# Score units inside the projections, four output chunks inside the score stream: one attention and feed-forward layer on one core

## The chip, the cores and the metric

The kernel runs on one core of a Trainium2 chip. The metric is the device time of one execution in microseconds (us): the median of three runs. Everything below that is not a median comes from one further execution, which the hardware profiler recorded.

## The reference

The input x has 2 sequences of 2048 rows and 256 channels; there are 16 heads of 16 channels. Cut to what matters:

```
q_in = x Wq' + b;  Q = [q_in, conv3(q_in)] proj_q' + b        # k likewise, V = x Wv' + b
tau, delta = sigmoid(conv1(gelu(depthwise_conv3(x))))         # one value per head and row
scores = (Q K' / 4) * tau + delta                             # 2 x 16 x 2048 x 2048
out    = softmax(scores) V;  x1 = layernorm(x + out Wo' + bo)
xq     = mxfp4_round(x1);    y  = layernorm(x1 + xq mxfp4_round(W)' + bf)
```

The rounding divides each block of 32 channels by a power of two taken from the block's largest value, clips to 6, rounds to a 4-bit float and multiplies back. It works on rows of x1, so a row needs all 16 heads first.

## The kernel before, in words

Rows are cut into 8 chunks of 512 (`NCHUNK`), chunks 0 to 3 of sequence 0 and 4 to 7 of sequence 1. Heads go in 8 groups of four (`NG`); an iteration is one group and one chunk of query rows, 32 iterations (`NIT`), those of sequence 1 from 16 on. Chunk n of the output is complete when its four groups are: chunk 3 with iteration 15, chunks 4, 5, 6 and 7 with iterations 28, 29, 30 and 31.

**The first block: projections** (`n` from 0 to 7). Convolution and projections are folded into one set of weights. For each chunk TensorE makes k in two halves, v in two, q in two (`project`, L608, 18 matmuls a half; `values`, L619), and the `pointwise` matmuls of tau and delta (L628) for the chunk after. VectorE adds the outer taps of the depthwise convolution (`tap`, L440), 16 instructions a chunk, between ScalarE's middle tap (L382) and gelu (L388). An fp32 operand is kept as a high part and a low part (`high`, `low`; L83 and L87): ScalarE writes the high parts of x, q and delta, VectorE the low ones (`split_low`, `q_lows` and one for delta). SyncE stores k, q and delta to DRAM and loads the first head group back.

**The score stream.** Softmax needs each row's maximum before its exponentials. So every score is made twice: once as a *unit*, a pair of matmuls into two PSUM banks (`s_unit`, L208) that VectorE reduces to maxima (`max_unit`, L218), and once transposed (`st`, L833) for ScalarE's exponential (L989) and the product with v (`pv_half`, L846). An iteration has 32 units. The list `items` holds all units in order, and after the third unit of each iteration one item `rows`, which turns the maxima of the iteration before (L820, L1024), for SyncE to store into `q_set` (`rows_store`, L797). Items use two pairs of banks in turn, so that item s waits on TensorE for the reduction of item s-2 (`s_free`). GpSimd splits the maxima (`split_max`).

Of `items`, `PRE_STEP` puts 28 into the projections of chunks 4 to 7; TensorE runs the next 17 at the start of the second block, each with six matmuls whose result nobody reads (L914), and only then the first `st`. From there, `due` items are spread over the 32 half-steps of an iteration, 33 in each of iterations 0 to 29 and 22 in the first 24 half-steps of iteration 30. I call a half-step a *slot*: one `pv_half`, one pair of `st`, and its item or items.

**Last iteration and tail.** From the third-last k tile of iteration 30 on, TensorE makes the output rows of chunks 0 to 3 (`project`, 16 *blocks* of 128 rows, L866 to L869). VectorE takes their layernorm statistics (`moments`, L1059, L1063), ScalarE a square root (L948), VectorE normalises (L1107) and rounds (`scales`, `steps`, `rounds`, L1080 to L1097). After the last `pv_half`, for n = 0 to 7: TensorE transposes the rounded chunk n (L884), projects chunk n+4, and multiplies with the feed-forward weights (`linear`, L904); ScalarE evacuates (`turn`, L971) and normalises twice (`norm`, L958). SyncE loads each chunk (`chunk_load`, L713 to L722: its rows of x, the attention of four groups, the reciprocals of the softmax sums) once the one two before has been used, and GpSimd multiplies the attention by the reciprocals (`normalise`, L1179). Every engine and every DMA queue takes its instructions in the order in which the code issues them.

```
for s in range(PRE, lead_in):
    s_item(s)
    for m in range(WARM):
        ...
issued = lead_in
for i in range(NIT):
    due = min(PER, len(items) - issued)
```

## Time and profile before

| | us |
|---|---|
| median of three runs | 1694.66 (1692.73 to 1697.91) |
| profiled execution, its own time | 1700.33 |
| its span, first to last instruction | 1698.5 |
| TensorE matmul busy | 1642.5 (97%) |
| VectorE busy | 1538.2 (91%) |
| ScalarE busy | 1322.7 (78%) |
| GpSimd busy | 74.6 (4%) |

How to read it: the profiled execution took 1.8 us outside its span, and is 5.7 us above the median. Shares of busy time are averages over stages with different limits. Times in rows are counted from the first instruction. The program has one core, and its mean granted TensorE clock is 0.981 of full speed.

### The profile page before, as it was taken

Reading aid. Unit: us, or ns where it says so; the run is one execution under the profiler, and the core shown is the slowest. Engines: PE = TensorE matmul, PEld = TensorE weight load, DVE = VectorE, ACT = ScalarE, POOL = GpSimd, SP = SyncE. Lnnn points to the kernel's source line nnn. Section 1 sums busy time; section 2 is a strip of 40 time slices with the busy share of each in tenths; the row PEclk is TensorE's granted clock in tenths of the full one; section 3 lists DMA queues with packets and bytes.
Section 4 is the critical chain, followed back from the end, with each engine's and each line's share of the span. In section 5 each row is a group of like instructions: output and inputs, shape, how many; then the busy total and the mean of one; then the engine's idle time right before and its main releaser. Section 6 shows DMA issues by size and latency. Waiting matters only on the chain.

```text
span 1698.5 us, 33654 instructions
## 1 busy us (share of the span) xinstructions
PE 1642.5 (97%) x13972; PEld 745.1 (44%) x13978; DVE 1538.2 (91%) x1638; ACT 1322.7 (78%) x2389; POOL 74.6 (4%) x133
## 2 busy tenths in 40 slices
PE   8999989999999999999999999999999999998977
PEld 7677754333333333333333333333333333334466
DVE  5588977999999999999999999999999999985797
ACT  3688723888888888888888888888888888885534
POOL 3000003000000000000000000000000000001110
PEclk9899997999999999999999999999999999999998
DMA  3376436000600060006002400322050000002232
GB/s 111 91 191 171 123 91 95 9 8 8 76 16 8 8 84 8 8 9 83 8 14 30 66 8 8 51 44 61 29 71 21 8 8 8 8 8 86 82 101 75
DMA packets 46961, 84.73 MB, mean 50 GB/s; under 512 B 9116, under 2 KB 21020, under 8 KB 44092
## 3 DMA queue, kind: packets, MB, share of 16 engines
q1 hardware_dynamic: 44952, 82.49, 22.6%
q8 instruction: 110, 1.80, 0.5%
q14 instruction: 43, 0.35, 0.1%
q10 hardware_dynamic: 1856, 0.09, 0.1%
HBM read 51.36 MB, written 30.67 MB: 48 GB/s over the span
## 4 chain that ended last, share of the span: by engine, by line
PE 62%; DVE 21%; ACT 1%; issue 1%; ACTq 0%; POOL 0%; DVEq 0%
PE ps L846 26%; PE ps L833 20%; DVE mx L218 17%; PE ps L208 11%; PE ps L869 1%; PE ps L914 1%; PE ps L867 1%; PE ps L820 0%; DVE stats L1059 0%; DVE work L1094 0%; DVE work L1093 0%; ACT e L989 0%; DVE work L1085 0%; DVE small L1080 0%; DVE scr L1089 0%
## 5 line engine op out<-in xcount | busy, mean ns | idle before, releaser
L218 DVE TENSOR_REDUCE mx<-ps 128x2 f32<-128x1024 f32 x1024 | 1230.4, 1223 | 60.6 <-PE ps L208 51.2
L989 ACT ACTIVATE e<-ps 128x512 f32<-128x512 f32 x2048 | 1110.3, 596 | 210.5 <-PE ps L833 170.4
L846 PE MATMUL ps<-e,v_grp 128*32 128x256 f32 x8192 | 657.7, 393 | 0.2 <-issue 0.2
L833 PE MATMUL ps<-q,k 52*128 52x512 f32 x2048 | 525.3, 499 | 4.0 <-ACT e L989 4.0
L208 PE MATMUL ps<-k,q 50*128 50x512 f32 x2048 | 420.8, 404 | 11.1 <-DVE mx L218 6.5
L833 PEld LDWEIGHTS ps<-q,k 52*128 52x128 f32 x2048 | 199.4, 184 | 430.8 <-ACT e L989 400.0
L846 PEld LDWEIGHTS ps<-e,v_grp 128*32 128x32 f32 x8192 | 162.1, 108 | 359.2 <-issue 202.4
L208 PEld LDWEIGHTS ps<-k,q 50*128 50x128 f32 x2048 | 198.9, 188 | 39.7 <-DVE mx L218 31.0
L608 PE MATMUL ps<-x_p,m_p 128*128 128x512 f32 x576 | 143.1, 405 | 0.0
L608 PEld LDWEIGHTS ps<-x_p,m_p 128*128 128x128 f32 x576 | 109.1, 193 | 31.0 <-issue 6.5
L440 DVE SCALAR_TENSOR_TENSOR hid<-x_c,dw_w,hid 128x512 f32<-128x512 f32 x128 | 88.5, 746 | 13.2 <-ACT hid L382 13.2
L388 ACT ACTIVATE hid<-hid 128x512 f32<-128x512 f32 x64 | 40.5, 633 | 41.4 <-DVE hid L440 40.0
L83 POOL CAST nm_pad<-nm 128x16 fp32r<-128x16 f32 x32 | 6.7, 209 | 923.1 <-DVE nm L1035 923.1
L382 ACT ACTIVATE hid<-x_c,dw_b,dw_w 128x512 f32<-128x512 f32 x64 | 46.6, 804 | 0.2
L1059 DVE BATCH_NORM_STATS2 stats<-ps 128x6 f32<-128x256 f32 x64 | 23.5, 419 | 21.9 <-PE ps L869 17.6
L869 PE MATMUL ps<-wo_t,v_all 128*128 128x256 f32 x128 | 36.7, 414 | 0.0
L628 PE MATMUL ps<-hid,pw_w 128*16 128x512 f32 x128 | 31.2, 594 | 0.2 <-ACT hid L388 0.2
L431 ACT ACTIVATE q_sp<-qx 128x512 fp32r<-128x512 f32 x16 | 10.1, 631 | 26.3 <-DVE qx L468 26.1
L619 PE MATMUL ps<-wv_p,x_p 128*128 128x256 f32 x192 | 27.1, 292 | 2.0 <-DVE v_all L458 2.0
L869 PEld LDWEIGHTS ps<-wo_t,v_all 128*128 128x128 f32 x128 | 26.8, 209 | 4.4
L958 ACT ACTIVATE o_sb<-ps,shift,rstd 128x256 f32<-128x256 f32 x32 | 15.5, 563 | 16.6 <-DVE shift L1071 16.6
L619 PEld LDWEIGHTS ps<-wv_p,x_p 128*128 128x128 f32 x192 | 25.7, 197 | 4.4 <-DVE v_all L458 2.1
(127 smaller groups left out, 621.8 us busy)
## 6 DMA issues: line engine op xcount, KB each, us to landing
k<-k_parts SPq DMA_DIRECT2D x42, 256.0 KB
q<-q_parts SPq DMA_DIRECT2D x42, 256.0 KB
k_parts<-k_sp SPq DMA_DIRECT2D x16, 512.0 KB, 5.1
q_parts<-q_sp SPq DMA_DIRECT2D x16, 512.0 KB, 4.6
att<-ev SPq DMA_DIRECT2D x32, 256.0 KB
x_c<-in_x_t SPq DMA_DIRECT2D x8, 514.0 KB, 6.4
tau_r<-tau_rows SPq DMA_DIRECT2D x16, 256.0 KB
x_in<-in_x SPq DMA_DIRECT2D x8, 512.0 KB, 3.7
```

Source lines behind the costliest of these rows:

```text
L208: last = nc.tensor.matmul(ps[:, s_bank(s) + half, :], q_set[r, g % 2, jh, lo + qt * P:lo + (qt + 1) * P], k_set[r, g % 2, jh, kc * CH:(kc ...
L218: nc.vector.tensor_reduce(mx[:, j % 2, :, jh, qt, kc], ps[:, b0:b0 + 2, :], AX.X, ALU.max).then_inc(s_free, 1)
L382: nc.scalar.activation(hid[:, k, c, r], x_c[:, n % 2, c, 1:1 + CH], ACT.Identity, bias=dw_b[:, k, c, r:r + 1], scale=dw_w[:, k, c, r, 1:2] ...
L388: nc.scalar.activation(hid[:, k, c, r], hid[:, k, c, r], ACT.Gelu).then_inc(gelu_done, 1)
L440: nc.vector.scalar_tensor_tensor(y_, x_c[:, n % 2, c, which:which + CH], dw_w[:, k, c, r, which:which + 1], y_, ALU.mult, ALU.add).then_in ...
L608: last = nc.tensor.matmul(ps[:, o, :], m_p[:, kw, side, c, tap, P * o:P * (o + 1)], x_p[:, n % 2, kx_, c, tap:tap + CH], start=(m == 0), s ...
L619: last = nc.tensor.matmul(ps[:, V_BANK, D * a:D * (a + 1)], x_p[:, n % 2, kx_, c, lo:lo + P], wv_p[:, kw, c, :], start=(m == 0), stop=(m = ...
L628: last = nc.tensor.matmul(ps[32 * k:32 * k + H, TD_BANK, :], pw_w[:, k, 2 * c + r, :], hid[:, k, c, r, :], start=(j < 2), stop=(j >= 6))
L833: nc.tensor.matmul(ps[:, st_bank(n), :], k_set[r, g % 2, jh, kt * P:(kt + 1) * P], q_set[r, g % 2, jh, lo:lo + CH], start=True, stop=True) ...
L846: last = nc.tensor.matmul(ps[32 * h:32 * (h + 1), 0, PVW * part:PVW * (part + 1)], v_grp[:, kt, h, :], e[:, x % E_BUFS, h * CH + PVW * par ...
L869: last = nc.tensor.matmul(dst, a_t[p][:, c, P * a:P * (a + 1)], wo_t[:, c, :], start=False, stop=(c == CT - 1))
L989: nc.scalar.activation(e[:, x % E_BUFS, h * CH:(h + 1) * CH], ps[:, st_bank(n), :], ACT.Exp).then_inc(e_ready, 1)
```

## The change

It does five things.

1. The units of iteration 0 are taken in another order (all of the first 512 keys, then the next 512, `place_of`), beginning in chunk 2; each group of 512 keys waits for its own loads. `PRE_STEP` now puts 42 items into the projections: 5 in chunk 2, 6 in each of chunks 3 to 6, and 13 in chunk 7, where they also stand between the matmuls of a half. The turn of iteration 0's maxima is among them. The separate lead-in of 17 items and its unread matmuls are gone: 14 go to the projections and 3 into iteration 0.
2. The low parts of x, q and delta are made by GpSimd.
3. The 16 blocks of chunks 0 to 3 become items: four in each of iterations 28 to 31 of the list, which the stream reaches in iterations 26 to 30. VectorE copies each from PSUM to `y_of`, and takes the statistics from there after the last item. Chunks 4 and 5 are projected in the last iteration in eight steps; chunks 6 and 7 after `linear(0)` and `linear(2)`.
4. ScalarE takes the square roots of chunks 0 to 3 together before the last iteration's first exponential, and a fourth set of softmax sums (`Z_SETS`) lets chunks 4 and 5 be loaded during iteration 31. Twenty unread matmuls stand at the end of iteration 30.
5. In chunk 0 the first values are evacuated after VectorE's other work, and the second ones have a bank of their own. SyncE waits for the stores of the first block in the second.

```diff
+        O_AT = {(28 + n, 8 * a + 5): ("o", n, a) for n in range(4) for a in range(TT)}
...
+        def place_of(j, u):
+            if j == 0:
+                return u % (HH * TT) // HH, u % HH, u // (HH * TT)
+            return u // (HH * NQ), u // NQ % HH, u % NQ
...
-        V_BANK, TD_BANK = 2, 3
+        v_bank = lambda n, v: 5 if (n, v) == (0, 1) else 2
...
-        PRE_STEP = {4: (0, 0, 0, 0, 0, 0, 2), 5: (0, 0, 1, 1, 1, 1, 1), 6: (0, 0, 1, 1, 1, 1, 1), 7: (2, 2, 2, 2, 2, 2, 4)}
+        PRE_STEP = {2: ONE_EACH(6, 9, 10, 13, 14)} | {n: ONE_EACH(5, 6, 9, 10, 13, 14) for n in range(3, 7)} | {7: [1] * 13 + [0, 0]}
...
+                for n in range(NCHUNK):
+                    if n + 1 < NCHUNK:
+                        split_low(n + 1)
+                    if n == NCHUNK - 1:
+                        split_max(pool, 0)
+                        pool.wait_ge(nm_ready, 1)
+                    pool.wait_ge(d_high, n + 1)
+                    low(nc.gpsimd, d_sp[32:32 + H, 1], td[32:32 + H], d_sp[32:32 + H, 0]).then_inc(d_split, 1)
...
+                    for o in range(CT):
+                        pool.wait_ge(q_high, CT * n + o + 1)
+                        low(nc.gpsimd, q_sp[:, o, 1], qx[:, o], q_sp[:, o, 0]).then_inc(q_split, 1)
...
-            PROJECT_AT = [LAST - 3, LAST - 3, LAST - 2, LAST - 2] + [LAST - 1 + m for m in range(3 * TT)]
-            ROOT_AT = {LAST + 1: 0, LAST + 5: 1, LAST + 10: 2}
+            PROJECT_AT = {x0 + a: (n, a) for n, x0 in ((4, LAST + 5), (5, LAST + 10)) for a in range(TT)}
+            ROOT_AT = {LAST - 1: range(EARLY)}
+            WARM_AT = (LAST - 2, LAST - 1)
...
+                            block_of(ps[:, s_bank(s), 0:D], n % 2, a).then_inc(s_full, 1)
...
+                        if s == len(items) - 1:
+                            pe.wait_ge(s_free, s - 1)
+                            unread(s_bank(s), 4)
...
-                    for s in range(PRE, lead_in):
-                        s_item(s)
-                        for m in range(WARM):
-                            for half in range(2):
-                                r = rows_of(half, K_S)
-                                nc.tensor.matmul(ps[:, st_bank(half), :], q_set[r, 0, 0, 0:P], k_set[r, 0, 0, 0:CH], start=True, stop=True)
...
-                        due = min(PER, len(items) - issued)
-                        slots = SLOTS if due == PER else SLOTS * 3 // 4
+                        goal = items.index((i + 2, LEAD)) if i + 2 < NIT else len(items) - 1
+                        due = goal - issued
+                        slots = SLOTS * 3 // 4 if i == NIT - 2 else SLOTS
...
                     for n in range(NCHUNK):
                         transposed(n)
-                        if n + EARLY < NCHUNK:
-                            for a in range(TT):
-                                project(n + EARLY, a)
                         linear(n)
+                        if n in (0, 2):
+                            for a in range(TT):
+                                project(6 + n // 2, a)
...
+                                nc.vector.tensor_copy(y_of[n][:, a], ps[:, s_bank(s), 0:D]).then_inc(s_free, 1)
...
+                        if i == NIT - 1:
+                            z_store(sp, 1)
+                            next_load(4)
+                            next_load(5)
                         if i > 0:
                             att_store(i - 1)
...
                     sp.wait_ge(att_stored, 32 * (NIT - 1))
-                    z_load(sp, 1)
-                    next_load(2)
-                    next_load(3)
-                    z_store(sp, 1)
-                    next_load(4)
-                    next_load(5)
+                    z_load(sp, 2)
+                    z_store(sp, 2)
                     att_store(NIT - 1)
                     next_load(6)
```

What this does to the order of instructions is shown at three places. The first is TensorE in the projections of chunk 3: the rows from one `pointwise` (16x512) to the next, before and with the change. `k,q` rows are score units.

```order
L628 MATMUL ps<-hid,pw_w 16x512 x8
L608 MATMUL ps<-x_p,m_p 128x512 x36
L619 MATMUL ps<-wv_p,x_p 128x256 x12
L608 MATMUL ps<-x_p,m_p 128x512 x18
L619 MATMUL ps<-wv_p,x_p 128x256 x12
L608 MATMUL ps<-x_p,m_p 128x512 x18
```

```order
L705 MATMUL ps<-hid,pw_w 16x512 x8
L225 MATMUL ps<-k,q 128x512 x2
L682 MATMUL ps<-x_p,m_p 128x512 x36
L225 MATMUL ps<-k,q 128x512 x2
L696 MATMUL ps<-wv_p,x_p 128x256 x12
L225 MATMUL ps<-k,q 128x512 x2
L682 MATMUL ps<-x_p,m_p 128x512 x18
L225 MATMUL ps<-k,q 128x512 x2
L696 MATMUL ps<-wv_p,x_p 128x256 x12
L225 MATMUL ps<-k,q 128x512 x2
L682 MATMUL ps<-x_p,m_p 128x512 x18
L225 MATMUL ps<-k,q 128x512 x2
```

A unit now follows each stage of the chunk; the work itself stands where it stood. The second place is VectorE in the same stage, from one group of four taps on its second half to q (`hid` are taps, `mx` reductions of units, L87 low parts): before in chunk 5, then with the change.

```order
L87 TENSOR_TENSOR x_p<-x_c,x_p 128x1028
L440 SCALAR_TENSOR_TENSOR hid<-x_c,dw_w,hid 128x512 x4
L218 TENSOR_REDUCE mx<-ps 128x2
L458 TENSOR_TENSOR v_all<-ps,bv_bc 128x32x16
L218 TENSOR_REDUCE mx<-ps 128x2
L440 SCALAR_TENSOR_TENSOR hid<-x_c,dw_w,hid 128x512 x4
L87 TENSOR_TENSOR d_sp<-td,d_sp 16x512
L468 SCALAR_TENSOR_TENSOR qx<-ps,side_bias,tau_r 128x512
L218 TENSOR_REDUCE mx<-ps 128x2
L468 SCALAR_TENSOR_TENSOR qx<-ps,side_bias,tau_r 128x512
L87 TENSOR_TENSOR q_sp<-qx,q_sp 128x512 x2
L218 TENSOR_REDUCE mx<-ps 128x2
```

```order
L523 SCALAR_TENSOR_TENSOR hid<-x_c,dw_w,hid 128x512 x4
L235 TENSOR_REDUCE mx<-ps 128x2
L537 TENSOR_TENSOR v_all<-ps,bv_bc 128x32x16
L235 TENSOR_REDUCE mx<-ps 128x2
L523 SCALAR_TENSOR_TENSOR hid<-x_c,dw_w,hid 128x512 x4
L547 SCALAR_TENSOR_TENSOR qx<-ps,side_bias,tau_r 128x512
L235 TENSOR_REDUCE mx<-ps 128x2
L547 SCALAR_TENSOR_TENSOR qx<-ps,side_bias,tau_r 128x512
L235 TENSOR_REDUCE mx<-ps 128x2
```

The four low parts have left VectorE; GpSimd has them in the order x (of the next chunk), delta, q, q. The third place is SyncE's queue around the end of iteration 31, with what each row waits for, with the change.

```order
L1313 DMA att<-ev 128x512 [waits att_evac]
L1315 DMA z_rows<-ev 4x512
L790 DMA x_in<-in_x 128x4x256 [waits o_full]
L795 DMA v_all<-att 64x1x512 x4
L799 DMA v_all<-rz_rows 128x1x512 [waits z_stored2]
L799 DMA v_all<-rz_rows 128x1x512
L775 DMA z<-z_rows 128x64 [waits att_stored]
```

The load of chunk 6 (L790 to L799) stands behind the store of iteration 31's result (L1313), as it did before; the loads of chunks 4 and 5 now stand well ahead of both. And at the same point TensorE's rows from the last matmuls of `linear(0)` (L988) on, with the change:

```order
L988 MATMUL ps<-fw_p,xq_t 128x256 [waits t_evac]
L988 MATMUL ps<-fw_p,xq_t 128x256 x7
L866 MATMUL ps<-bias,ones 128x256 [waits y_ready,a_norm,x_in_loaded0]
L867 MATMUL ps<-x_in,ident_f 128x256
L869 MATMUL ps<-wo_t,v_all 128x256 x2
```

The first block of chunk 6 (L866 to L869; three more follow) stands right behind `linear(0)`, ahead of the transposition of chunk 1, and waits for its own load (`a_norm`).

## Rows read from the trace of the kernel before

**Rows 1.** By stage: length, busy PE, PEld, DVE, ACT, POOL; clock, DMA share, GB/s
```profile
74.50:247.70 173.20, 171.80 (x816) 122.87 (x816) 143.58 (x201) 121.71 (x171) 0.00 (x0) 1.00 0.54 145
256.20:275.90 19.70, 19.49 (x133) 13.74 (x135) 17.59 (x18) 1.28 (x1) 14.34 (x25) 0.89 0.45 82
275.90:1529.00 1253.10, 1247.67 (x11855) 466.14 (x11853) 1200.53 (x1060) 1083.74 (x2006) 25.96 (x91) 0.99 0.18 28
1529.00:1604.50 75.50, 68.40 (x504) 34.33 (x496) 48.46 (x88) 47.33 (x83) 11.70 (x5) 0.98 0.27 87
1604.50:1698.50 94.00, 68.01 (x382) 57.84 (x384) 77.52 (x187) 35.07 (x79) 7.11 (x3) 0.87 0.25 85
```

**Rows 2.** Timeline around chunk 0: start, length, engine, line [idle before, releaser]
```profile
58.94 0.69 DVE L458 TENSOR_TENSOR v_all<-ps,bv_bc 128x512 f32<-128x512 f32 x1 [12.51 <-POOL v_all L352]
59.69 2.93 PE L619 MATMUL ps<-wv_p,x_p 128*128 128x256 f32 x12 [1.97 <-DVE v_all L458]
...
74.51 8.66 PE L608 MATMUL ps<-x_p,m_p 128*128 128x512 f32 x36
```

**Rows 3.** TensorE's timeline: starts of chunks 2, 3, 5 and 6
```profile
97.89 8.65 PE L608 MATMUL ps<-x_p,m_p 128*128 128x512 f32 x36
121.23 8.67 PE L608 MATMUL ps<-x_p,m_p 128*128 128x512 f32 x36
...
168.63 8.68 PE L608 MATMUL ps<-x_p,m_p 128*128 128x512 f32 x36
...
194.78 8.65 PE L608 MATMUL ps<-x_p,m_p 128*128 128x512 f32 x36
```

**Rows 4.** VectorE's groups: count, busy us and mean ns
```profile
L440 DVE SCALAR_TENSOR_TENSOR hid<-x_c,dw_w,hid 128x512 f32<-128x512 f32 x128 | 88.5, 746 | 13.2 <-ACT hid L382 13.2
...
L87 DVE TENSOR_TENSOR x_p<-x_c,x_p 128x1028 fp32r<-128x1028 f32 x8 | 9.8, 1225 | 1.2 <-ACT x_p L376 1.2
```

**Rows 5.** GpSimd and VectorE at the same time, timeline
```profile
1570.38 2.36 POOL L1179 TENSOR_TENSOR v_all<-v_all 128x1024 f32<-128x1024 f32 x1 [6.64 <-DMA v_all<-rz_rows]
1570.81 3.01 DVE L1085 TENSOR_TENSOR work<-y,small 128x1024 f32<-128x1024 f32 x1
```

**Rows 6.** TensorE in the stream: starts of a single slot, a double one and the next
```profile
1251.63 0.64 PE L846 MATMUL ps<-e,v_grp 128*32 128x256 f32 x8
...
1252.87 0.64 PE L846 MATMUL ps<-e,v_grp 128*32 128x256 f32 x8
...
1254.69 0.64 PE L846 MATMUL ps<-e,v_grp 128*32 128x256 f32 x8
```

**Rows 7.** TensorE: first and second block of chunk 0 (first matmul of each)
```profile
1533.15 0.28 PE L866 MATMUL ps<-bias,ones 128*128 128x256 bf16 x1
...
1534.57 0.27 PE L866 MATMUL ps<-bias,ones 128*128 128x256 bf16 x1
```

**Rows 8.** TensorE in iteration 31: two slots of a k tile without block, next tile
```profile
1597.95 0.64 PE L846 MATMUL ps<-e,v_grp 128*32 128x256 f32 x8
...
1598.95 0.64 PE L846 MATMUL ps<-e,v_grp 128*32 128x256 f32 x8
...
1600.18 0.64 PE L846 MATMUL ps<-e,v_grp 128*32 128x256 f32 x8
```

**Rows 9.** ScalarE's timeline: the first of two table loads around a root
```profile
1544.96 1.28 ACT L948 ACT_TABLE_LOAD   x1
```

**Rows 10.** The last chunk's load: SyncE's first DMA, GpSimd, TensorE's first block
```profile
1633.69 0.43 SPq L713 DMA_DIRECT2D x_in<-in_x  x1
...
1646.22 2.35 POOL L1179 TENSOR_TENSOR v_all<-v_all 128x1024 f32<-128x1024 f32 x1 [16.53 <-DMA v_all<-rz_rows]
...
1639.39 0.36 PE L866 MATMUL ps<-bias,ones 128*128 128x256 bf16 x1 [4.71 <-ACT y L958]
...
1646.91 1.03 PE L898 MATMUL ps<-v_all,ident_f 128*128 128x256 f32 x4
```

**Rows 11.** Busy time in the stretch at half clock after the first exponentials
```profile
281.00:294.00 13.00, 13.00 (x76) 4.24 (x79) 7.39 (x7) 6.67 (x13) 0.00 (x0) 0.50 1.03 122
```

More of the change, by code:

```diff
@@ L633, in pre_scores @@
                     for s in pre_at.get((n, place), ()):
-                        s_unit(pe, s)
+                        if items[s][1] == "rows":
+                            rows_turn(pe, s)
+                        else:
+                            s_unit(pe, s)
                 beta(1, 0)
@@ L802, in _, with block_of, loaded, unread @@
                 def _(pe):
+                    def block_of(dst, p, a):
+                        nc.tensor.matmul(dst, ones3[:], bias3[:, 0, 0, :], start=True, stop=False)
+                        nc.tensor.matmul(dst, ident_f[:], x_in[:, p, a, :], start=False, stop=False)
+                        for c in range(CT):
+                            last = nc.tensor.matmul(dst, a_t[p][:, c, P * a:P * (a + 1)], wo_t[:, c, :], start=False, stop=(c == CT - 1))
+                        return last
+                    def loaded(n):
+                        pe.wait_ge(x_in_loaded[n % 2], 16 * (n // 2 + 1))
+                        pe.wait_ge(a_norm, n + 1)
+                    def unread(bank, pairs):
+                        for m in range(pairs):
+                            for half in range(2):
+                                r = rows_of(half, K_S)
+                                nc.tensor.matmul(ps[:, bank + half, :], q_set[r, (NG - 1) % 2, 0, 0:P], k_set[r, (NG - 1) % 2, 0, 0:CH], start=True, stop=True)
                     def s_item(s):
                         j, u = items[s]
+                        if isinstance(u, tuple):
+                            n, a = u[1:]
+                            pe.wait_ge(s_free, s - 1)
+                            if a == 0:
+                                loaded(n)
+                            if (n, a) == (0, 0):
+                                pe.wait_ge(bias_ready, 1)
+                            block_of(ps[:, s_bank(s), 0:D], n % 2, a).then_inc(s_full, 1)
+                            return
                         if u == "ft":
@@ L931, in _ @@
                                     issued += 1
[L932 to L935 removed]
+                                if i == NIT - 2 and 2 * k + jh == slots:
+                                    s_item(len(items) - 1)
+                            if x in PROJECT_AT:
+                                project(*PROJECT_AT[x])
+                            if x in WARM_AT:
+                                pe.wait_ge(s_free, len(items))
+                                unread(4, 3)
                     for n in range(NCHUNK):
                         transposed(n)
[L939 removed]
+                        linear(n)
+                        if n in (0, 2):
                             for a in range(TT):
[L941 to L942 removed]
+                                project(6 + n // 2, a)
                 @block.scalar
@@ L1138, in _ @@
+                    for n in range(6, NCHUNK):
+                        moments(1, n)
                         scale_shift(1, n)
@@ L1195, in _ @@
                                 refill(g + 1, c)
-                    for n in range(NCHUNK):
+                    for n in range(EARLY, NCHUNK):
                         normalise(n)
```

407 lines of the change are left out of this document (232 added, 175 removed).

## The prediction, made before the changed kernel was run

> **What bounds the kernel now.** I read the stages first, in the answer that sums each engine's work by stretch [rows 1]. In the projections (74.5 to 247.7) TensorE is busy 171.8 of 173.2 us and VectorE 143.6: TensorE sets the pace. Then comes the lead-in, 19.7 us before the first exponential. In the stream VectorE has 1200.5 of 1253.1 us and TensorE 1247.7, so both are full. From 1529.0, the copy of the last maxima, to the last product with v at 1604.5, VectorE works 48.5 of 75.5 us. In the tail of 94.0 us it works 77.5, the most of any engine. Next I took the starts of TensorE's pieces from the timeline, since a start to start distance holds the waits. A slot with one item takes 1.24 us, one with two 1.83 [rows 6], of which I put 0.15 down to a wait for VectorE, whose two reductions fall into one slot there (my choice; no row splits it). 31 x 1.24 + 1.83 = 40.3 is one iteration. VectorE has 33 items of 1.22 there, some 40.0 in all. What is added to TensorE in the stream therefore shows in full, and what is taken from VectorE does not.
>
> **Chunk 0.** VectorE stands 12.5 us before the first values, and TensorE 2.0 behind it [rows 2]. Both waits go. TensorE gains at least the 2.0. VectorE's taps for chunk 1 come some 6 us sooner, so the last tau and delta matmuls stop waiting for gelu. I take chunk 1 to start at 70.8 instead of 74.5. Ends: 72.5 and 69.5.
>
> **Units in the projections.** A chunk without units takes 121.2 - 97.9 = 23.3 us, one with five 194.8 - 168.6 = 26.15 [rows 3], so a unit costs 0.57. Chunk 7 ran with 14 units from 220.9 (one chunk after 194.8) to 247.7, 26.8 us; with 13 some 26.3. Chunk 1 then ends at 94.1, chunk 2 at 120.2, chunks 3 to 6 take 4 x 26.7 and end at 227.0, chunk 7 at 253.3. One q evacuation, one high and one low part, and the change of block follow, 3.4 us. The first `st` comes at 256.7 instead of 275.9: **-19.2**. Three items move to iteration 0, each between 0.6 (TensorE, 1.83 - 1.24) and 1.22 (VectorE); I take 1.0, as VectorE is nearer to its limit there: **+3.0**.
>
> The units are hidden from VectorE only if it keeps up. A chunk costs it some 19.3 us without units, 16 x 0.746 of it taps. The low parts go: x 1.23 [rows 4], and by their columns 0.7 each for delta and both q, 3.3 together. Six reductions of 1.17 to 1.22 come: 23.2 of 26.7. GpSimd gets them in return. Its two-input instruction over 1024 columns takes 2.36 us [rows 5], so a chunk gives it about 2.4 + 3 x 1.3 = 6.3. When it ran at 1570.4, VectorE's instruction with two SBUF inputs took 3.01 us instead of 1.2 and ended 1.1 after GpSimd's [rows 5]: it had stood still. VectorE's 16 taps have two SBUF inputs too. By the order of the streams x's low part falls on reductions and evacuations, delta's on the second taps, q's on reductions. I take 2 us a chunk as lost, which the 3.5 of slack hold. The Trainium skill, SBUF — State Buffer, section Who interferes with whom, says it as a rule: a VectorE instruction with two SBUF inputs and a GpSimd one that reads SBUF exclude each other for their whole length, a reduction never. By that rule, with all overlaps at their worst, this change would lose time; the trace agrees with the exclusion.
>
> **Blocks in the stream.** A block is 1534.57 - 1533.15 = 1.42 us of TensorE [rows 7], and VectorE's copy of 256 columns some 0.4. 16 x 1.42 = 22.7. The items push others together: 37 items in 32 slots make five double slots instead of one, four times the difference between 1.68 and 1.24 less what four slots without unit save (1.00 instead of 1.24, [rows 8]), about 0.8 an iteration; together 2.8 over the iterations 26 to 30: **+25.5**. Low end 22.7. High end: after a block VectorE has at most one item waiting, and stands up to 2.1 us until the next unit; at 16 x 2.1 it is 34. Five more unread pairs and one slot before the last turn of maxima, of which TensorE waited 1.2 for GpSimd anyway: **+1.8**. The last copy of maxima then ends 11.1 us later than now, at 1540.1.
>
> **From there to the last product.** Now it is 75.5 us. With the change ScalarE takes four roots before iteration 31's exponentials. VectorE needs 1.0 for the reciprocals and four times 1.8 for statistics, so the last root comes at 8.4 and, after a table load of 1.28 [rows 9], the first exponential at 9.7 after the copy. TensorE stops at 5.3, when the three banks of `st` are full, and goes on at 10.3. The end of iteration 30 with its unread matmuls, partly at half clock after the stop, reaches 16.7. Iteration 31 has 14 k tiles of 2.23 [rows 8], two of 1.05 and eight blocks of 1.5: 45.5. Sum 62.2: **-13.3**. VectorE has rounded chunks 0 to 3 by 64.9; it waits some 7 us in it for chunks 4 and 5.
>
> **The tail.** VectorE starts one chunk ahead of where it is now, but new waits eat this. The load of chunk 6 is issued after iteration 31's result is stored, 1.8 us after the last product. From a load's first DMA to GpSimd's product are 12.5 us, that takes 2.35, four blocks after an idle time 7.5 [rows 10], transposition and `linear(1)` 4.5. So the statistics of chunk 1 are due 28.6 us into the tail, where VectorE arrives at 20: what is late next is that load. Chunk 7's blocks stand behind the normalised chunk 6 and ahead of `linear(3)`: another 5. With two waits of 2 us for `norm`, the chunks 4 to 7 need 17 + 21 + 22 + 17 = 77 us from 2.7 on, and the last feed-forward chain 13.4: 93.1 instead of 94.0, **-0.9**.
>
> Sum: -19.2 + 3.0 + 25.5 + 1.8 - 13.3 - 0.9 = -3.1. I round to **-4**, because in chunk 0 the clock may return sooner when TensorE is not idle. The profiled execution would go from 1700.3 to about 1696 (span 1694.5); it stood 5.7 above the median, so the median is 1694.7 - 4 = **1690.5**. A measurement of this kernel can tell 0.3%, 5.1 us, from no change, so this is just inside.
>
> **Rivals.**
> - *The tail has no new waits* (chance 0.20). If the load lands sooner, or VectorE arrives later, the idle 8.6 and 5 go: -4 - 14 = -18, 1677. For it: VectorE does work 77.5 of 94 us now. Against it: the measured 12.5 us of the load.
> - *VectorE and GpSimd exclude each other in the projections* (0.12), slower. If all 6.3 us of GpSimd stop taps, VectorE's chain of taps, gelu, tau and delta, middle taps (some 25 us) becomes 31.5 instead of the 26.7 of TensorE: 4.8 in each of five chunks, +24, net +20, 1711 to 1715. It decides from 4 us a chunk on. For it: 3.01 instead of 1.2. Against it: most of GpSimd's work falls on reductions.
> - *Blocks cost VectorE's time as well* (0.10): the high end of 34, net +4.5, 1699.
> - *The clock* (0.08). For 13 us after the first exponentials it is granted at 0.50, the lower of its two levels, 1.2 GHz [rows 11], and the tail's mean is 0.87 [rows 1]. TensorE stops for 3.4 us at 253 and 5 at 1545. If it stays at 1.2 GHz longer than now, 5 to 12 us are lost: 1695 to 1703. It could also be shorter by 5.
> - *The change does not do what it says*: if units in the projections waited for VectorE instead of filling in, the lead-in would only have moved. That is the second rival in another form, and has its price.
>
> **How the numbers follow.** The sum's case has 0.50, from -10 to +2 by the ends of chunk 0, the units and the blocks: 0.21 of it faster by over 0.3%, 0.27 within, 0.02 slower. The others add 0.20, 0 and 0; 0, 0 and 0.12; 0, 0.06 and 0.04; 0.03, 0.01 and 0.04. Together faster 0.44, same 0.34, slower 0.22. The range 1672 to 1706 takes in the first rival with the better ends of the sum, the third and the clock, and leaves out most of the second. The sum's own range is 1684 to 1697.
>
> **What would show it.** First `st` near 257, TensorE gapless in chunks 1 to 7 and 26.7 a chunk; iterations 27 to 29 of 47 us instead of 40.3; the last copy of maxima near 1540; last product 62 after it; then VectorE idle for 8 us before the statistics of chunk 1. A chunk of 28 or more, with TensorE waiting for gelu or a reduction, would prove the exclusion. Wrong would be a tail under 85 us, or blocks that cost 1.0 or 2.0 each.

## The result: 1% slower, and the profile after

| | before | changed |
|---|---|---|
| median of nine runs, us | 1695.94 (1692.73 to 1705.17) | 1715.56 (1708.43 to 1723.67) |
| ratio | 1 | 1.0098, 95% interval 1.0069 to 1.0127 |
| the same, timed again with the experiments | 1 | 1.0071, 1.0045 to 1.0097 |
| span of the profiled execution | 1698.5 | 1713.8 |

By the two ratios the kernel became slower by 12 to 17 us, where 4 us were forecast as a gain; its median of 1715.56 us lies above the end of the range that I gave, 1706. Busy time by stage of the changed kernel, cut at the places that answer to those of before [rows 1]; the columns are the same, and the gap between the two blocks has a line of its own. The stages are: the start of chunk 1 to the last projection; the gap; the first score to the last copy of maxima; from there to the last product with v; and the tail:

```profile
71.76:255.90 184.14, 184.12 (x852) 125.56 (x851) 154.30 (x191) 120.69 (x170) 45.10 (x30) 1.00 0.50 137
255.90:259.70 3.80, 0.00 (x0) 0.03 (x1) 0.88 (x2) 2.12 (x3) 1.30 (x2) 0.94 0.34 92
259.70:1548.07 1288.37, 1282.06 (x11987) 487.45 (x11987) 1204.80 (x1078) 1084.55 (x2008) 48.64 (x117) 0.99 0.18 32
1548.07:1618.13 70.06, 65.11 (x451) 27.70 (x444) 56.06 (x120) 41.17 (x77) 5.21 (x2) 0.78 0.17 52
1618.13:1713.80 95.67, 55.23 (x329) 46.13 (x328) 62.69 (x156) 35.63 (x78) 4.71 (x2) 0.84 0.24 81
```

Read it against the forecast. TensorE is without a gap in the projections (184.12 of 184.14), as forecast. The stream takes 1288.4 instead of 1253.1: 35.3 more, where 30.3 were forecast. The stage behind it has a mean clock of 0.78 where it had 0.98 before, and takes 70.1 us instead of the forecast 62.2. VectorE has 15 us less work in the tail than before, and the tail is still 1.7 us longer.

The starts of chunks 3, 4 and 5 in TensorE's timeline [rows 3 for before]:

```profile
148.10 8.66 PE L682 MATMUL ps<-x_p,m_p 128*128 128x512 f32 x36
174.85 8.70 PE L682 MATMUL ps<-x_p,m_p 128*128 128x512 f32 x36
201.69 8.66 PE L682 MATMUL ps<-x_p,m_p 128*128 128x512 f32 x36
```

26.8 us for a chunk with six units, forecast 26.7. VectorE's taps in the group of that line [rows 4 for before]:

```profile
L523 DVE SCALAR_TENSOR_TENSOR hid<-x_c,dw_w,hid 128x512 f32<-128x512 f32 x128 | 103.8, 862 | 21.2 <-ACT hid L464 21.2
```

They take 0.862 instead of 0.746 us each, 15.3 us in all or 1.9 a chunk. In one chunk, VectorE's timeline shows it in a single place:

```profile
213.22 1.22 DVE L235 TENSOR_REDUCE mx<-ps 128x2 f32<-128x1024 f32 x1
214.35 4.59 DVE L523 SCALAR_TENSOR_TENSOR hid<-x_c,dw_w,hid 128x512 f32<-128x512 f32 x4
```

GpSimd's timeline at the same time:

```profile
212.96 2.41 POOL L87 TENSOR_TENSOR x_p<-x_c,x_p 128x1028 fp32r<-128x1028 f32 x1 [10.36 <-ACT x_p L458]
215.45 1.62 POOL L87 TENSOR_TENSOR d_sp<-td,d_sp 16x512 fp32r<-16x512 f32 x1
```

Four taps take 4.59 us where four others of the chunk take 2.87, and until 217.07 GpSimd writes the low parts of x and of delta beside them. The exclusion is there, at the 2 us a chunk that I had put down, and it is hidden.

A block in the stream, in TensorE's timeline and then in VectorE's (the last block of chunk 0, [rows 7] for a block before):

```profile
1443.17 0.28 PE L866 MATMUL ps<-bias,ones 128*128 128x256 bf16 x1
1443.29 0.60 PE L867 MATMUL ps<-x_in,ident_f 128*128 128x256 f32 x2
1443.73 1.03 PE L869 MATMUL ps<-wo_t,v_all 128*128 128x256 f32 x4
1444.68 0.64 PE L936 MATMUL ps<-e,v_grp 128*32 128x256 f32 x8
...
1444.79 0.42 DVE L1114 COPY y<-ps 128x256 f32<-128x256 f32 x1 [1.27 <-PE ps L869]
1446.03 2.36 DVE L235 TENSOR_REDUCE mx<-ps 128x2 f32<-128x1024 f32 x2 [0.82 <-PE ps L225]
```

The block takes TensorE 1.5 us (1443.17 to 1444.68), and VectorE stands 1.27 before its copy and 0.82 behind it. In the whole iteration (1415.24 to 1462.93) VectorE works 39.6 of 47.7 us and TensorE 47.3, so TensorE sets the pace. By ScalarE's copies of a finished iteration (1367.56, 1415.24, 1462.93, 1510.66), iterations 27 to 29 take 47.7 us each, against 40.3 without blocks.

The worst place is the end of the stream. ScalarE's timeline, and TensorE's at the same time:

```profile
1548.79 3.27 ACT L1070 ACTIVATE e<-ps 128x512 f32<-128x512 f32 x6 [1.39 <-PE ps L923]
1552.08 1.28 ACT L1030 ACT_TABLE_LOAD   x1
1553.37 0.48 ACT L1030 ACTIVATE std<-mv,eps_col 128x4 f32<-128x4 f32 x2
1554.04 0.30 ACT L1030 ACTIVATE std<-mv,eps_col 128x4 f32<-128x4 f32 x1 [0.18 <-DVE mv L1165]
1555.74 0.30 ACT L1030 ACTIVATE std<-mv,eps_col 128x4 f32<-128x4 f32 x1 [1.40 <-DVE mv L1165]
1556.06 1.28 ACT L1070 ACT_TABLE_LOAD   x1
```

```profile
1552.87 0.50 PE L923 MATMUL ps<-q,k 52*128 52x512 f32 x1
1558.00 0.79 PE L923 MATMUL ps<-q,k 52*128 52x512 f32 x1 [4.62 <-ACT e L1070]
1558.00 2.07 PE L882 MATMUL ps<-k,q 50*128 50x512 f32 x6
```

ScalarE loads a table, takes four roots (the last waits for VectorE's statistics) and loads the table back: 5.3 us. TensorE stops for 4.62 us at the score matmul that needs a free bank. Of the twenty unread matmuls, twelve stand behind that score matmul in the program and come after the stop (the first six at 1558.00). Two stretches in which TensorE runs at the lower clock (same columns as the stages):

```profile
260.00:278.00 18.00, 17.74 (x90) 6.17 (x90) 7.22 (x6) 10.56 (x20) 10.85 (x19) 0.50 0.86 165
1558.00:1585.60 27.60, 27.60 (x154) 8.87 (x155) 26.56 (x38) 16.03 (x30) 5.21 (x2) 0.50 0.31 94
```

In the second, 27.6 us long, the granted clock is 0.50, the lower level of 1.2 GHz, while TensorE is busy without a gap. It stays there until 1587.0, which is 29.0 us after the stop. The first stretch, behind the first score, lasts from 259.3 to 279.8. Neither was in my sum at this length. What the lower level costs is seen in the starts of two k tiles of iteration 31: 3.47 us apart at 0.50 (1566.48 and 1569.95). At 1.00 it was 2.23 before [rows 8], and 2.24 in e2 below (1558.85 and 1561.09).

In the tail, TensorE's two long waits, SyncE's two entries about the load of chunk 6, and GpSimd's product of chunk 6 [rows 10 for before]:

```profile
1634.71 0.37 PE L866 MATMUL ps<-bias,ones 128*128 128x256 bf16 x1 [11.40 <-POOL v_all L1286]
...
1663.62 0.37 PE L866 MATMUL ps<-bias,ones 128*128 128x256 bf16 x1 [12.36 <-ACT y L1039]
```

```profile
1618.83 0.32 SPq L1313 DMA_DIRECT2D att<-ev  x1
...
1619.78 0.45 SPq L790 DMA_DIRECT2D x_in<-in_x  x1
...
1632.27 2.34 POOL L1286 TENSOR_TENSOR v_all<-v_all 128x1024 f32<-128x1024 f32 x1 [54.88 <-DMA v_all<-rz_rows]
```

The load starts 1.65 us after the last product with v (forecast 1.8), GpSimd's product of it is done at 1634.6, and everything behind it on TensorE is queued. VectorE then waits 7.68 us before its statistics of chunk 1, and later 6.14 before those of chunk 3:

```profile
1645.88 1.65 DVE L1162 BATCH_NORM_STATS2 stats<-ps 128x6 f32<-128x256 f32 x4 [7.68 <-PE ps L988]
```

### The profile page after: what moved, and what is told of

It reads as the page before. It is cut to its first block, busy times and chain, and to the rows that moved or that the text cites. A ratio compares the mean times of both kernels' runs of the same rounds, so it can differ in the third digit from the quotient of the medians.

```text
span 1713.8 us, 33544 instructions
## 1 busy us (share of the span) xinstructions
PE 1650.1 (96%) x13896; PEld 734.7 (43%) x13896; DVE 1522.4 (89%) x1622; ACT 1317.8 (77%) x2386; POOL 127.2 (7%) x166
## 4 chain that ended last, share of the span: by engine, by line
PE 62%; DVE 21%; ACT 1%; issue 1%; DMA 1%; SPq 0%; POOL 0%; ACTq 0%
PE ps L936 26%; PE ps L923 20%; DVE mx L235 18%; PE ps L225 11%; PE ps L869 2%; PE ps L867 1%; DVE stats L1162 1%; DMA v_all<-rz_rows 1%; PE ps L242 0%; PE ps L866 0%; PE ps L988 0%; PE ps L982 0%; ACT o_sb L1039 0%; DVE mv L1165 0%; DVE work L1195 0%
## 5 line engine op out<-in xcount | busy, mean ns | idle before, releaser
L235 DVE TENSOR_REDUCE mx<-ps 128x2 f32<-128x1024 f32 x1024 | 1227.9, 1223 | 79.6 <-PE ps L225 71.8
L936 PE MATMUL ps<-e,v_grp 128*32 128x256 f32 x8192 | 664.9, 396 | 0.6 <-issue 0.5
L523 DVE SCALAR_TENSOR_TENSOR hid<-x_c,dw_w,hid 128x512 f32<-128x512 f32 x128 | 103.8, 862 | 21.2 <-ACT hid L464 21.2
L1162 DVE BATCH_NORM_STATS2 stats<-ps 128x6 f32<-128x256 f32 x48 | 17.6, 420 | 29.1 <-PE ps L988 16.8
L1262 POOL COPY v_grp<-v_all 128x272 f32<-128x272 f32 x32 | 13.4, 426 | 316.0 <-PE ps L936 316.0
L869 PE MATMUL ps<-wo_t,v_all 128*128 128x256 f32 x128 | 35.6, 404 | 0.0
L866 PE MATMUL ps<-bias,ones 128*128 128x256 bf16 x32 | 9.6, 299 | 23.8 <-ACT y L1039 12.4
L1286 POOL TENSOR_TENSOR v_all<-v_all 128x1024 f32<-128x1024 f32 x8 | 19.4, 2428 | 132.6 <-DMA v_all<-rz_rows 132.6
L869 PEld LDWEIGHTS ps<-wo_t,v_all 128*128 128x128 f32 x128 | 26.5, 207 | 4.3
L696 PE MATMUL ps<-wv_p,x_p 128*128 128x256 f32 x192 | 26.5, 287 | 0.0
```

What stands on the lines that cost most here:

```text
L235: nc.vector.tensor_reduce(mx[:, j % 2, :, jh, qt, kc], ps[:, b0:b0 + 2, :], AX.X, ALU.max).then_inc(s_free, 1)
L523: nc.vector.scalar_tensor_tensor(y_, x_c[:, n % 2, c, which:which + CH], dw_w[:, k, c, r, which:which + 1], y_, ALU.mult, ALU.add).then_in ...
L869: last = nc.tensor.matmul(dst, a_t[p][:, c, P * a:P * (a + 1)], wo_t[:, c, :], start=False, stop=(c == CT - 1))
L936: last = nc.tensor.matmul(ps[32 * h:32 * (h + 1), 0, PVW * part:PVW * (part + 1)], v_grp[:, kt, h, :], e[:, x % E_BUFS, h * CH + PVW * par ...
L1162: last = nc.vector.bn_stats(stats[:, k, p, a], src)
```

## The experiments

Three theories stood at the start. *The clock*: the stop at 1553 is followed by some 29 us at half clock. *Order in the tail*: the load of chunk 6 and the place of chunk 7's blocks. *The rival*: the low parts on GpSimd cost time after all. Each was undone alone, with the rest as changed. Ratios are to the kernel before, timed on the same chip.

**e1, the roots two k tiles later.**

```diff
-            ROOT_AT = {LAST - 1: range(EARLY)}
+            ROOT_AT = {LAST + 1: range(EARLY)}
```

> The changed kernel with ScalarE's four square roots two k tiles later (after the exponentials of tile 1 of the last iteration instead of the tile before it). Theory, the clock: TensorE's stop of 4.6 us at 1553 is what lets the granted clock fall to 0.50 until 1586. Then the stop shrinks to under 1.5 us, the clock stays at 1.00 through the last iteration, and the kernel is 12 to 17 us faster than the changed one (ratio to the kernel before 1.001 to 1.005). Rival, the stop only: the clock falls there anyway, whatever TensorE did before; then 3 to 4 us. Second rival: the roots late hold VectorE up, whose four roundings come 3 to 14 us later, and the tail gives the gain back.

Measured 1.0046 (1.0029 to 1.0063). In TensorE's timeline and by stretch:

```profile
1553.55 0.79 PE L923 MATMUL ps<-q,k 52*128 52x512 f32 x1 [2.84 <-ACT e L1070]
```

```profile
1552.00:1576.00 24.00, 22.45 (x118) 7.50 (x118) 23.10 (x33) 13.82 (x25) 4.72 (x2) 0.50 0.25 86
```

My expectation missed. ScalarE's two table loads and four roots (3.4 us) go on stopping TensorE, for 2.84 us, and the clock falls as before, for 24 us. The stop became shorter, not harmless, so this run does not tell the two theories apart. By the ratios 4 to 9 us are won, where 12 to 17 were expected.

**e2, the stop filled.**

```diff
-            WARM_AT = (LAST - 2, LAST - 1)
+            WARM_AT = ()
...
+                            if (x, jh, half) == (LAST, 1, 1):
+                                pe.wait_ge(s_free, len(items))
+                                unread(4, 17)
                             if n >= ST_BUFS:
                                 pe.wait_ge(e_ready, n - ST_BUFS + 1)
```

> The changed kernel with TensorE's stop kept and filled: 17 pairs of unread matmuls (4.6 us at full clock) directly ahead of the score matmul that waits for ScalarE, and the twelve unread ones behind it left out. Theory, the clock: it stays at 1.00 although ScalarE's pause is as long as before, and 12 to 16 us are won. Rival, the pause of ScalarE itself costs: the clock stays, but less than 4 us are won. Rival, the clock falls anyway: nothing is won, as the unread matmuls only move.

Measured 1.0013 (0.9991 to 1.0034). TensorE's timeline, then the stage from the last copy of maxima to the last product:

```profile
1548.31 4.36 PE L882 MATMUL ps<-k,q 50*128 50x512 f32 x34
1553.40 0.50 PE L926 MATMUL ps<-q,k 52*128 52x512 f32 x1 [0.73 <-ACT e L1073]
```

```profile
1543.46:1602.01 58.55, 56.99 (x473) 27.92 (x466) 56.01 (x121) 40.41 (x77) 5.14 (x2) 1.00 0.21 62
```

ScalarE's pause is as long as before, but TensorE now waits 0.73 us with nothing to do, and the clock stays at 1.00. The stage takes 58.6 us instead of 70.1, and 10 to 14 us are won by the ratios. So it is not ScalarE's pause that costs, but what follows a stop of TensorE. Most of that is the half clock: a k tile takes 3.47 us at 0.50 and 2.24 at 1.00, so I estimate 29.0 x (1 - 2.24 / 3.47) = 10.3 us for it. The twelve unread matmuls that e2 leaves out behind the stop would be another 1.5, at the 0.13 us that each takes here (4.36 / 34). Together the estimates are 11.8, and the two stages are 11.5 us apart. The Trainium skill, TensorE: Matmul & The Clock Gate, section Terms, puts the penalty at the time spent at the lower clock times one half; by that the 29.0 us would cost an estimated 14.5. The trace agrees in kind but not in size, for a k tile at the lower level takes 1.55 times as long here, not twice.

**e3, the load of chunk 6 ahead of the last store.**

```diff
+                    next_load(6)
                     att_store(NIT - 1)
-                    next_load(6)
```

> The changed kernel with the load of chunk 6 issued before the store of iteration 31's result instead of behind it. Theory, the load is what the start of the tail waits for: GpSimd's product of chunk 6 comes before 1620, TensorE's wait of 11.4 us ahead of chunk 6's blocks goes, and the tail is 8 to 10 us shorter. Rival, VectorE's own work sets the tail: TensorE's wait goes, but VectorE's idle time only moves, and the gain is under 3 us.

Measured 1.0012 (0.9989 to 1.0035). The tail by stretch, and TensorE's blocks of chunks 6 and 7:

```profile
1612.66:1700.90 88.24, 54.99 (x330) 45.70 (x328) 62.80 (x156) 35.79 (x78) 2.34 (x1) 0.85 0.21 70
```

```profile
1618.17 0.27 PE L866 MATMUL ps<-bias,ones 128*128 128x256 bf16 x1 [0.33 <-ACT v_all L1039]
...
1649.51 0.37 PE L866 MATMUL ps<-bias,ones 128*128 128x256 bf16 x1 [14.58 <-ACT y L1039]
```

The wait of 11.4 us is 0.33 now, and the tail 88.2 instead of 95.7 to 96.8: 8 us, where 8 to 10 were expected. The ratios give 10 to 15; what lies beyond the tail was not placed. The next wait, for chunk 6 to leave bank 4, grew from 12.4 to 14.6.

**e4, the low parts on VectorE.** The edit moves `split_low`, the low part of delta and those of q back into VectorE's stream, at the places that they have in the kernel before.

> The changed kernel with the low parts of x, delta and q on VectorE as in the kernel before, all else as changed. Theory, GpSimd's help is needed and its price small: VectorE has 19.3 + 3.3 + 7.2 = 29.8 us in a chunk with six units, so chunks 3 to 7 take 28 to 29.5 instead of 26.8, TensorE waits for gelu or q, and the kernel is 5 to 13 us slower than the changed one; the taps come back from 0.86 to 0.75 us. Rival, exclusion: GpSimd's instructions cost VectorE more than they save; then this one is faster than the changed kernel.

Measured 1.0075 (1.0049 to 1.0102), the same as the changed kernel. VectorE's taps from the start of chunk 1 on (96 of the 128):

```profile
L506 DVE SCALAR_TENSOR_TENSOR hid<-x_c,dw_w,hid 128x512 f32<-128x512 f32 x96 | 67.1, 751 | 12.3 <-ACT hid L447 12.3
```

The taps come back to 0.751 us, but the chunks stay at 26.8 (starts at 143.16, 169.91, 196.74). Neither theory holds: GpSimd's help is not needed, and its price is not paid. My expectation had a slip of its own, for the 19.3 us of VectorE's work already held the low parts, so the sum is 26.5, not 29.8. The trace shows less still: VectorE works 25.0 of the 26.8 us from 169.91 to 196.74.

**c0, the changed kernel again.** No edit.

> The changed kernel itself, timed once more beside the experiments of this call, as their control. Both theories: 1.008 to 1.011 of the kernel before. The profile may come out several us apart from the first one, because the stretches at half clock were 12 to 33 us long behind the same stop in four executions.

Measured 1.0071 (1.0045 to 1.0097), just under the 1.008 to 1.011 expected. The last two stages:

```profile
1553.18:1616.12 62.94, 57.98 (x451) 26.72 (x444) 55.88 (x121) 40.82 (x77) 5.79 (x2) 0.92 0.20 58
1616.12:1712.90 96.78, 55.22 (x329) 46.10 (x328) 62.68 (x156) 35.67 (x78) 4.70 (x2) 0.82 0.25 80
```

The stop is the same 4.62 us, but the half clock lasted only 9.3 us behind it here (to 1572.4), so this stage takes 62.9: less than 1 us above my forecast. Over the seven profiles that have the stop of 4.6 us, the stage is either 62.9 to 63.0 us (three) or 70.0 to 70.9 (four).

**e5, the gap between the blocks filled.**

```diff
+                pe.wait_ge(s_free, PRE - 1)
+                for m in range(11):
+                    for half_ in range(2):
+                        r = rows_of(half_, K_S)
+                        nc.tensor.matmul(ps[:, s_bank(PRE - 2) + half_, :], q_set[r, 0, 0, 0:P], k_set[r, 0, 0, 0:CH], start=True, stop=True)
```

> The changed kernel with 22 unread matmuls (3.0 us) at the end of TensorE's first block, in the 3.8 us between the last projection and the first score, where TensorE stood still. Theory, the clock: the 10 to 20 us at half clock that follow the first exponential go, and 4 to 9 us are won. Rival, the clock falls with the first exponentials whatever TensorE did before (in the kernel before it falls at 281 in the midst of steady work): nothing is won.

Measured 1.0073 (1.0045 to 1.0101), no gain. TensorE's timeline, and the clock behind it:

```profile
255.75 2.79 PE L747 MATMUL ps<-k,q 50*128 50x512 f32 x22
259.66 0.70 PE L928 MATMUL ps<-q,k 52*128 52x512 f32 x3 [1.12 <-PEq L353]
```

```profile
262.50:275.00 12.50, 12.50 (x78) 4.08 (x80) 6.07 (x5) 7.29 (x15) 4.98 (x11) 0.59 0.84 174
```

A gap of 1.12 us is left, and the first score runs at full clock (0.70 instead of 1.19 for its first matmuls), but at 262.7 the clock falls all the same, for 10.2 us. Here the rival has it: this fall does not need a long stop. What starts it stays open.

**e6, thin blocks.**

```diff
-                            block_of(ps[:, s_bank(s), 0:D], n % 2, a).then_inc(s_full, 1)
+                            nc.tensor.matmul(ps[:, s_bank(s), 0:D], ones3[:], bias3[:, 0, 0, :], start=True, stop=True).then_inc(s_full, 1)
```

> The changed kernel with one matmul (the bias, 0.28 us) in place of the seven of each of the 16 blocks in the stream: their x and their product with wo are left out; VectorE's copies and all waits stay. Theory, a block costs TensorE's time and 0.4 more: iterations 27 to 29 take 43 us instead of 47.7, and the kernel is 16 to 20 us faster than the changed one. Rival, a block costs through the two score banks and VectorE's copy: iterations take 45 us or more, and under 12 us are won.

This kernel leaves out six of the seven matmuls of each block, so its output is not the layer's; it serves to price them. Measured 0.9937 (0.9916 to 0.9958), by the ratios 23 to 27 us under the two measurements of the changed kernel, where 16 to 20 were expected. One iteration with four thin blocks:

```profile
1404.51:1447.15 42.64, 42.21 (x391) 16.13 (x389) 39.36 (x39) 35.13 (x66) 3.06 (x4) 1.00 0.14 45
```

42.6 us instead of 47.7: a block costs 1.86 us ((47.7 - 40.25) / 4, by an iteration without blocks), of which 1.27 are the six matmuls left out here and 0.59 is what stays: the item and its one matmul. Sixteen times 1.27 is 20.3 us, the most of the gain. The first theory holds: blocks are mostly paid in TensorE's time. VectorE works 39.4 of the 42.6 us.

**e8, chunk 7's blocks behind the linear of chunk 3.**

```diff
-                        if n in (0, 2):
+                        if n in (0, 3):
                             for a in range(TT):
-                                project(6 + n // 2, a)
+                                project(6 + n // 3, a)
```

> The changed kernel with chunk 7's blocks behind the linear of chunk 3 instead of chunk 2. Theory, order: TensorE waits 12.4 us there for chunk 6 to leave the bank, with chunk 3's linear queued behind it, and VectorE then waits 6.1 us for that linear; both waits shrink, and 4 to 7 us are won in the tail. Rival, VectorE's statistics of chunk 7, which now come later than it wants them, make a wait of the same length: under 2 us won.

Measured 1.0038 (1.0013 to 1.0064). The tail:

```profile
1604.36:1696.80 92.44, 55.79 (x329) 46.60 (x328) 62.80 (x156) 35.74 (x78) 4.69 (x2) 0.84 0.25 84
```

92.4 instead of 95.7 to 96.8 in the tail, so 3 to 4 us come from the order, a little under the 4 to 7 expected. The ratios give 6 to 10 us; the rest is not explained.

**b0, the kernel before again.** No edit.

> The kernel before, profiled a second time. Theory: its executions differ as well, through the stretches at half clock behind the lead-in and in the tail; the stream from the first score to the last copy of maxima stays at 1253, from there to the last product at 75 to 76, the tail at 93 to 95, and what is apart from the first profile lies ahead of the stream and in its first iteration.

Measured 1.0013 (0.9994 to 1.0031). Its three stages from the first score on:

```profile
276.93:1523.37 1246.44, 1241.17 (x11853) 463.69 (x11849) 1200.42 (x1060) 1083.72 (x2006) 26.00 (x91) 1.00 0.18 28
1523.37:1601.99 78.62, 71.51 (x504) 35.53 (x496) 48.55 (x88) 47.58 (x83) 11.04 (x5) 0.91 0.27 83
1601.99:1698.10 96.11, 67.18 (x378) 57.09 (x384) 77.87 (x187) 35.02 (x79) 7.18 (x3) 0.90 0.26 84
```

The stream takes 1246.4 us here, not the 1253.1 of [rows 1]: the 13 us at half clock after the first exponentials [rows 11] are missing from this execution. In exchange the next two stages are 3.1 and 2.1 us longer. In the first of them the clock is at 0.50 for 6.8 us from 1524.3 on, 1.5 us behind a wait of 1.22; the same wait in the first profile was followed by none. All three stages lie outside what I had expected of them. So a stage of the first profile is not a fixed number, even where the span is.

**e9, three mends together:** e2, e3 and e8.

> The changed kernel with three mends together: the stop ahead of the last iteration filled with unread matmuls, the load of chunk 6 ahead of the store of iteration 31, chunk 7's blocks behind the linear of chunk 3. Theory, the three are separate places: 58.6 us from the last copy of maxima to the last product and a tail of 84 to 88, so 0.997 to 1.001 of the kernel before. Rival, VectorE's own work in the tail (70 us and the last chain) becomes the bound: a tail of 88 or more, and 1.001 to 1.004.

Measured 0.9959 (0.9938 to 0.9980), a little under the range expected and 0.4% faster than the kernel before. Its last two stages:

```profile
1545.72:1604.23 58.51, 56.98 (x473) 27.70 (x466) 56.37 (x114) 40.41 (x77) 7.49 (x3) 1.00 0.29 89
1604.23:1689.60 85.37, 55.35 (x324) 46.62 (x328) 64.32 (x162) 35.77 (x78) 2.34 (x1) 0.87 0.21 72
```

58.5 and 85.4 us instead of 70.1 and 95.7. The places are separate, and together they turn +1% into -0.4%.

**e11, the first half of the change alone.** The program up to the end of the first block is the changed one, with no blocks among the items (`O_AT = {}`) and the three sets of softmax sums; the second block is the kernel before's, without its lead-in.

> The changed kernel's first half (units from chunk 2 on, no lead-in, low parts on GpSimd, chunk 0's order) with the second half of the kernel before: chunks 0 to 3 projected in the last iteration, roots one by one, four softmax sets back to three. Theory, the first half of the change gains and the second loses: the first score at 256 to 259 instead of 276, three items more in the stream (3 us), last iteration and tail as in the kernel before; 13 to 17 us faster than the kernel before, 0.990 to 0.993. Rival, what the first half gains comes back at half clock in the first iteration: 0.995 or more.

Measured 0.9923 (0.9897 to 0.9949), from six runs, as expected: faster than both kernels, and the lowest ratio of the study. Its three stages:

```profile
258.29:1515.50 1257.21, 1251.52 (x11857) 467.43 (x11857) 1201.55 (x1061) 1083.06 (x2006) 40.16 (x114) 0.99 0.18 30
1515.50:1594.19 78.69, 71.57 (x504) 35.63 (x496) 48.33 (x87) 47.58 (x83) 12.89 (x5) 0.91 0.26 83
1594.19:1687.80 93.61, 65.36 (x378) 55.60 (x384) 76.53 (x187) 35.08 (x79) 7.32 (x3) 0.91 0.26 86
```

The first half gains. The first score comes 18.6 us sooner than in b0, and the last copy of maxima 7.9 us sooner: of the 10.8 us that the stream is longer, 3.1 lie behind the first iteration and 7.7 in it (from the first score to ScalarE's first copy of a finished iteration 50.5 us against 42.8), where the clock was at 0.50 for some 17 us. Where the 3.1 come from was not found. The second half of the change is what loses.

**e12, e11 with the low parts on VectorE.**

> The kernel of e11 (first half as changed, second half as before) with the low parts of x, delta and q on VectorE. Theory, the low parts on GpSimd move nothing: the chunk pitch stays at 26.8 us, TensorE stays gapless in chunks 1 to 7, and the ratio to the kernel before is within 0.003 of e11's 0.992. Rival, VectorE without that relief is just at its limit, and chunks 3 to 7 take 28 us: 0.995 or more.

Measured 0.9949 (0.9926 to 0.9973). The chunks are 26.8 us again (145.25, 171.99, 198.83), with VectorE at 163.0 of 183.5 us between 66.5 and 250. The intervals of e11 and e12 overlap, and e12's profiled execution was the shorter of the two (span 1680.5 against 1687.8), so whether GpSimd's part is worth anything is not shown; the two intervals together put it between -0.1% and 0.6%. The chunks did not lengthen to 28 us, so the rival falls.

## Where the prediction went wrong, point by point

Each step of the sum, beside the two profiles of the changed kernel (us):

| step | forecast | first profile | c0 |
|---|---|---|---|
| start of chunk 1 | 70.8 | 71.8 | 71.1 |
| first score | 256.7 | 259.7 | 259.0 |
| first score to last copy of maxima | 1283.4 | 1288.4 | 1294.2 |
| from there to the last product | 62.2 | 70.1 | 62.9 |
| tail | 93.1 | 95.7 | 96.8 |
| sum | 1695.4 | 1713.8 | 1712.9 |

The sum misses by 18.4 us in the first profile and by 17.5 in c0, but not at the same places: the first score, the stream, the last iteration and the tail miss by 3.0, 5.0, 7.9 and 2.6 us in the first, and by 2.3, 10.8, 0.7 and 3.7 in c0. Two slips of 0.2 us stand in the forecast beside this: iteration 31's terms add up to 45.3, and 1694.7 - 4 is 1690.7. The first score of the kernel before comes at 276.2, 0.3 us behind the cut at 275.9 that I took for it.

**Right.** The projections: TensorE gapless, 26.8 us a chunk, the start of chunk 1 within 1 us, and the first score: in the nine profiles that run the changed kernel's first block unaltered it comes at 255.8 to 259.7, with the forecast 256.7 inside. The six units and the taps together kept VectorE at 23.3 to 23.7 us a chunk (chunks 5 and 6), where I had 23.2, and 2 more for the exclusion. The exclusion of VectorE and GpSimd: seen in the taps, 1.9 us a chunk against the 2 that I took, and hidden; so that rival fell by its own condition, which asked for 4. The stop of TensorE: forecast from 5.3 to 10.3 us after the copy, measured from 5.3 to 9.9. The late load of chunk 6 and VectorE's wait for the statistics of chunk 1: due at 28.6 us in the tail by the forecast, 27.8 by the trace (1645.88).

**The step that failed first** is "The end of iteration 30 with its unread matmuls, partly at half clock after the stop, reaches 16.7. Iteration 31 has ... 45.5", with iteration 31 at full clock. I let the clock come back within about 6 us after the stop. In the seven profiles with this stop of 4.6 us it stayed at 0.50 for 9 to 31 us behind it, although TensorE was busy, and the stage took 63 or 70 us; filled, it takes 58.5. In the first profile 7.9 us of the miss lie here. In c0 only 0.7 do; there the same assumption failed in iteration 0, which had three more items in my sum and no longer stretch at half clock than before: the clock stayed at 0.50 for 33.4 us behind the first score, and the iteration took 57.4 us, 5.4 more than its place in my sum (324.9 - 275.9 + 3.0). The fourth rival, the clock, named both stops and 5 to 12 us, and I gave it 0.08. The profile had shown that such a stretch can be long [rows 11]: 13 us at half clock in the midst of steady work. A range for it belonged in the sum. It could not have been one price for every stop, for in the kernel before a stop of 3.6 us in iteration 31 is followed by 3.4 us at half clock in the first profile and by 4.6 in b0. What decides the length was not found.

**Blocks: mis-sized a little.** The forecast was 25.5 + 1.8 = 27.3. From ScalarE's first copy of a finished iteration to the last copy of maxima, the two profiles of the changed kernel take 1236.1 and 1236.8 us and e11 1206.8: 29 to 30. The 0.8 us an iteration for items that push others together was too little; a block costs 1.86, not 1.6. The high end of 34 for the blocks held it. Against the kernel before (1204.2 and 1203.6) the same stretch is 32 to 33 longer, so 4.7 and 5.3 us of the miss lie here, some 3 of them in what e11 has as well.

**The first half: the clock took a part of what it gave.** The -19.2 was -16.2 in the first profile, -16.9 in c0 and -18.6 for e11 against b0. But the half clock behind the first score, 9 to 33 us long in all twelve profiles that have the new order of units, falls into full work there. In the two of before a stretch of 10 us began ahead of the lead-in, and a second one, of 13.7 us behind the first exponentials, came in one of them only. First score to the first finished iteration took 47.6 to 57.4 us in the twelve, against 42.8 and 48.7 in the two of before.

**The distance to the median.** I carried 5.7 us over from the profile of before to the median. The changed kernel's profile stands on its own median (its execution took 1715.56), so this accounts for 5.7 of the 25 us by which the median was missed; 18.4 are the table's, and 0.9 the rounding.

**The tail: right causes, wrong sum.** It was 95.7 to 96.8 us instead of 93.1. The load and the order of chunk 7's blocks were named, with 8.6 and 5 us as VectorE's waits (measured 7.7 and 6.1); not in the sum were the stretches at half clock behind TensorE's two long waits. e3 and e8 take away 8 and 4.

In all: moving the blocks costs 29 to 30 us in the stream, where TensorE is full, and gives back 4 to 16 behind it (62.9 or 70.1, against 73.8 to 78.7 in the four profiles with the old second half) and nothing in the tail (95.7 and 96.8, against 93.6 to 96.1). The first half gains 8 us up to the last copy of maxima (b0 against e11) and 13 by e11's ratio. My forecast had the two halves within 4 us of each other, so the stretches at half clock alone were enough to turn the sign (7.9 us in the first profile, about 6 in c0), and the blocks and the tail added to it.

## What to carry to other kernels

Price a stop of TensorE by the stretch at half clock that can follow, as a range, and not by its own length: here the stage behind a stop of 4.6 us took 4 to 12 us more than with the stop filled. Unread matmuls helped when they stood in the program *ahead of* the instruction that waits (e2); the twelve behind it ran at half clock. Before work is moved into a stage in which TensorE is full, make sure that the work that it leaves behind was on the path to the end; sixteen blocks of 1.86 us went in here, and what came back behind them was about half of it at most. And where a profile is compared with a forecast stage by stage, take two profiles of before: the stages of two differed here by 2 to 7 us, and the spans by 0.4.

## What the runs showed of the hardware that was not expected

- The granted clock stayed at 0.50 for 27.6 us with TensorE busy for 27.60 of them. How long it stays differs from execution to execution of the same program: 29.0 us behind the stop of 4.6 us in the first profile, 9.3 behind the same stop in c0. In the seven profiles with that stop it is 9.3 to 9.5 or 29 to 31 us.
- A stop of 2.84 us was followed by 22.4 us at 0.50 (e1), one of 0.73 by none (e2), and the wait of 1.22 us at the end of the stream in the kernel before by 6.8 us in one execution and by none in the other.
- At 0.50 a k tile of iteration 31 took 3.47 us instead of 2.24, which is 1.55 times as long.
- The clock also falls 3.0 us after the first score with a gap of only 1.12 us before it (e5), and in the kernel before some 5 us after it, in one execution of two. The cause of this fall was not found.
